# The causal convolution folded into the input projection on TensorE, and the routing weights computed on GpSimd, in a macaron block of MoE, Mamba and MoE

## The reference, cut to what matters

```
# FFN: 8 experts of 176 hidden, 2 per token, and a shared one of 352
router = xf @ Wg;  top_logits, idx = top_k(router, 2);  probs = softmax(top_logits)
w = zeros(n, 8).at[arange, idx].add(probs)
y = einsum('eth,ehc,te->tc', silu(xf W1) * (xf W2), W3, w) + (silu(xf Ws1) * (xf Ws2)) Ws3

# Mamba: inner width 256, state 16, 4 taps
xz = x @ W_in + b_in;  x_in, z = split(xz)
xt = causal_depthwise_conv(x_in, conv_w) + conv_b          # padded with 3 zeros on the left
x_conv = silu(xt)
Bm, Cm = split(x_conv @ W_xp + b_xp);  delta = softplus(x_conv @ W_dt + b_dt)
h = exp(delta*A) * h + delta*x_conv*Bm;  y = sum_s(h*Cm) + D_skip*x_conv
out = (y * silu(z)) @ W_out + b_out;  return layernorm(x + out) * alpha + beta
```

## Time and profile before

| | before |
|---|---|
| median of 3 runs | 2298.14 us (2297.28 to 2298.89) |
| the profiled execution | 2294.5 us, span 2292.7 us |
| mean granted clock of TensorE | 0.859 |
| busy: PE, DVE, ACT, POOL | 77%, 80%, 68%, 63% |
| instructions | 22561 |
| DMA | 299.53 MB, mean 131 GB/s |

### The profile page before, as it was taken

One profiled execution on the slowest core, in us unless ns is written; L12 is line 12 of the kernel. 1 busy time (PEld: TensorE's weight loads), 2 busy tenths in 40 slices (PEclk: granted clock), 3 DMA queues, 4 the chain that ended last, 5 costly groups with the idle time before them and its releaser, 6 DMA issues.

```text
span 2292.7 us, 22561 instructions
## 1 busy us (share of the span) xinstructions
PE 1759.5 (77%) x4416; PEld 770.7 (34%) x4416; DVE 1834.1 (80%) x2628; ACT 1554.5 (68%) x2114; POOL 1452.1 (63%) x1284
## 2 busy tenths in 40 slices
PE   4858488878788777787878787788778878876577
PEld 2323133333333333333333333333333333323233
DVE  1378989788897988979788897978979788888742
ACT  2449487776778677767776777777677867776522
POOL 3256676666576666666666666666666666676753
PEclk9879689788898889889898898988889888887688
DMA  4126655545554555546555554555455455546641
GB/s 127 51 79 152 143 137 150 136 121 132 145 139 124 148 133 142 130 122 161 133 129 133 135 139 122 144 139 133 124 139 149 127 143 132 132 118 166 151 106 60
DMA packets 118986, 299.53 MB, mean 131 GB/s; under 512 B 19168, under 2 KB 40384, under 8 KB 104512
## 3 DMA queue, kind: packets, MB, share of 16 engines
q0 software_dynamic: 18432, 125.84, 27.4%
q1 hardware_dynamic: 92672, 168.88, 23.3%
q10 hardware_dynamic: 7744, 3.57, 0.6%
HBM read 167.15 MB, written 5.24 MB: 75 GB/s over the span
## 4 chain that ended last, share of the span: by engine, by line
DVE 31%; PE 26%; ACT 18%; issue 18%; POOL 4%; DMA 1%; ACTq 1%; DVEq 1%; POOLq 0%
DVE hist L847 10%; PE ps_y L1027 6%; DVE ps_db L813 4%; PE ps_h2a L1032 4%; ACT L668 4%; ACT L645 3%; DVE dtmp L923 3%; PE ps_h1a L1014 3%; DVE den L891 3%; PE ps_h1b L1014 3%; PE ps_h2b L1032 2%; ACT decay L645 2%; DVE yacc L950 2%; ACT silu L668 2%; PE ps_m L1074 2%
## 5 line engine op out<-in xcount | busy, mean ns | idle before, releaser
L560 POOL TENSOR_TENSOR prod<-hist,crow 128x1024 f32<-128x1024 f32 x224 | 558.1, 2492 | 390.8 <-DVE hist L847 388.7
L847 DVE TENSOR_TENSOR_SCAN hist<-decay,ps_db 128x1024 f32<-128x1024 f32 x256 | 583.4, 2279 | 15.4 <-issue 12.8
L1027 PE MATMUL ps_y<-gated,down_w 128*128 128x512 f32 (+1 forms) x896 | 517.6, 664 | 96.0 <-POOL gated L512 64.0
L512 POOL TENSOR_TENSOR gated<-gated,silu 128x512 f32<-128x512 f32 x352 | 473.7, 1408 | 134.6 <-DVE gated L839 104.9
L813 DVE TENSOR_TENSOR ps_db<-du,ps_db 128x1024 f32<-128x1024 f32 x256 | 313.4, 1224 | 192.1 <-PE ps_db L996 190.0
L645 ACT ACTIVATE decay<-delta,a_neg 128x510 f32<-128x510 f32 x512 | 338.3, 711 | 2.6
L1032 PE MATMUL ps_h2a<-xnT,up_w 128*128 128x512 f32 (+1 forms) x448 | 259.2, 663 | 57.0 <-DVE gated L839 57.0
L1014 PE MATMUL ps_h1a<-xnT,up_w 128*128 128x512 f32 (+1 forms) x448 | 259.6, 663 | 50.0 <-ACT silu L668 48.8
L668 ACT ACT_TABLE_LOAD x229 | 293.8, 1283 | 5.3 <-PE ps_h1a L1014 1.2
L1032 PE MATMUL ps_h2b<-xnT,up_w 128*128 128x512 f32 x448 | 250.3, 642 | 53.6 <-DVE gated L839 53.6
L1027 PEld LDWEIGHTS ps_y<-gated,down_w 128*128 128x128 f32 (+1 forms) x896 | 181.6, 210 | 321.4 <-issue 211.9
(11 more groups left out here) (127 smaller groups left out, 2377.7 us busy)
## 6 DMA issues: line engine op xcount, KB each, us to landing
yacc<-prod POOLq DMA_DIRECT2D x112, 1024.0 KB, 8.9
crow<-c_rows SPq DMA_DIRECT2D x128, 512.0 KB, 4.1
wrow<-w_rows SPq DMA_DIRECT2D x320, 128.0 KB, 3.3
wrow<-w_rows SPq DMA_DIRECT2D x64, 224.0 KB, 3.1
wrow<-w_rows SPq DMA_DIRECT2D x64, 192.0 KB, 3.2
wrow<-w_rows SPq DMA_DIRECT2D x64, 160.0 KB, 3.2
yacc<-yacc POOLq DMA_DIRECT2D x16, 512.0 KB, 6.2
wrow<-w_rows SPq DMA_DIRECT2D x64, 96.0 KB, 3.0
```

What stands on the lines that cost most here:

```text
L512: nc.gpsimd.tensor_tensor(gated[:, pos % NGATE, :], gated[:, pos % NGATE, :], silu[:, (pos + NCHUNK * f_parity(k, f)) % NSILU, :], ALU.mul ...
L560: nc.gpsimd.tensor_tensor(prod[:, (pair - 1 + odd) % 2, s % 2, :, :], hist[:, s % 2, :, :], c_all, ALU.mult).then_inc(prod_done, 1)
L847: nc.vector.tensor_tensor_scan(hist[:, s % 2, :, :].rearrange("p h t -> p (h t)"), decay[:, s % NA, :, :, :].rearrange("p h b t -> p (h b ...
L1027: nc.tensor.matmul(ps_y[:], down_w[0:rd, jd, :], gated[0:rd, posd % NGATE, :], start=(posd == 0), stop=(posd == NCHUNK - 1)).then_inc(down ...
```

## The change

1. The four taps are folded into the weights of the input projection: at the start VectorE makes `w_conv[:, tap, :]` = `W_in` times the tap of each channel. `in0` and `in1` are then four matmuls each over the normed input, shifted by 0 to 3 tokens, that accumulate in `ps_m`, and a fifth over six columns that takes the bias of `b_in` back out where the padding stands. ScalarE's silu reads `ps_m` and writes `xconv`. The steps `conv0a` to `conv1b`, `xin` and the copy to it are gone; `dt0` and `xproj` wait for `in1` having been taken.
2. `weights0` and `weights1` run on GpSimd in the same slots, between the gated product and the state product of the slot; the reciprocal is a power of -1.
3. `wT` and `cT` become one buffer, `bounce`, to make room; each copy into it waits for the other's store.
4. At the start there are one more constant transfer (the taps, broadcast), six small operations on VectorE, two transposes and a copy for the fifth matmul's weights.

```diff
-        10: ["wT0", "conv0a"], 11: ["outT", "conv0b"], 12: ["resid"], 13: ["in1", "stats3"], 14: ["in2", "conv1a"],
-        15: ["in3", "conv1b", "ln_norm"], 17: ["y1"], 18: ["dt0", "stats1"], 19: ["dt1"], 20: ["yT1", "norm1"],
+        10: ["wT0"], 11: ["outT"], 12: ["resid"], 13: ["in1", "stats3"], 14: ["in2"],
+        15: ["in3", "ln_norm"], 17: ["y1"], 18: ["dt0", "stats1"], 19: ["dt1"], 20: ["yT1", "norm1"],
...
-        cT = sb("cT", [NS, TG])
+        bounce = sb("bounce", [NS, TG])
+        wT, cT = bounce[0:E, :], bounce
...
+                        elif step == "weights0" and enters(k) or step == "weights1" and tail(k):
...
+                            pool.wait_ge(edrop_ready, n + 1)
+                            chain.link(nc.gpsimd.tensor_tensor(den[:], edrop[:], pow_mone[:], ALU.subtract))
+                            chain.link(nc.gpsimd.tensor_tensor(prob[:, :, 0], den[:], pow_mone[:], ALU.pow))
+                            chain.link(nc.gpsimd.tensor_tensor(prob[:, :, 1], edrop[:], prob[:, :, 0], ALU.mult))
+                            pool.wait_ge(hot_ready, n + 1)
+                            chain.link(nc.gpsimd.tensor_tensor(
+                                hotp[:].rearrange("p t i e -> p (t i) e"), hot[:].rearrange("p t i e -> p (t i) e"),
+                                prob[:].rearrange("p t i -> p (t i)").unsqueeze(2).to_broadcast([P, TILES * 2, E]),
+                                ALU.mult))
+                            nc.gpsimd.tensor_tensor(wtok[:], hotp[:, :, 0, :], hotp[:, :, 1, :], ALU.add
+                                                    ).then_inc(wtok_ready, 1)
...
+                            held = k + 2 if step == "wT1" and lead(k) else k + 1
+                            if not isinstance(k, int) or 0 < held <= G:
+                                act.wait_ge(c_stored, 16 * held)
+                            nc.scalar.activation(wT, ps_m[0:E, :], ACT.Copy).then_inc(misc_taken, 1)
...
-                            nc.scalar.activation(xin[:, half, :, PAD:PAD + LEN],
-                                                 ps_m[:].rearrange("p (b t) -> p b t", b=NSEQ), ACT.Identity,
-                                                 bias=b_in_c[:, half:half + 1]).then_inc(misc_taken, 1)
+                            nc.scalar.activation(xconv[nxt][:, half, :], ps_m[:], ACT.Silu,
+                                                 bias=b_conv[:, half:half + 1]).then_inc(misc_taken, 1)
...
+            taps = taps_b.rearrange("p (c t) -> p t c", t=TAPS)
+            nc.vector.tensor_tensor(w_conv[:], w_in[:, 0:DI].unsqueeze(1).to_broadcast([P, TAPS, DI]), taps, ALU.mult
+                                    ).then_inc(taps_made, 1)
...
+            def convolved(half):
+
+                now = xnT[2][:].rearrange("p (b t) -> p b t", b=NSEQ)
+                acc = ps_m[:].rearrange("p (b t) -> p b t", b=NSEQ)
+                for tap in reversed(range(TAPS)):
+                    late = PAD - tap
+                    nc.tensor.matmul(acc[:, :, late:LEN], w_conv[:, tap, half * P:(half + 1) * P],
+                                     now[:, :, 0:LEN - late], start=(tap == PAD), stop=False)
+                return nc.tensor.matmul(acc[:, :, 0:PAD], edge_w[:, half * P:(half + 1) * P], edge[:],
+                                        start=False, stop=True)
...
-                            nc.tensor.matmul(ps_m[:], w_in[:, c * P:(c + 1) * P], xnT[2][:], start=True, stop=True
-                                             ).then_inc(misc_full, 1)
+                            if c < HALVES:
+                                convolved(c).then_inc(misc_full, 1)
+                            else:
+                                nc.tensor.matmul(ps_m[:], w_in[:, c * P:(c + 1) * P], xnT[2][:], start=True, stop=True
+                                                 ).then_inc(misc_full, 1)
```

More of the change, by code:

```diff
@@ L260, in macaron_kernel @@
         yT = sb("yT", [P, TG])
-        xin = sb("xin", [P, HALVES, NSEQ, PAD + LEN])
+        w_conv = sb("w_conv", [P, TAPS, DI])
+        b_tap = sb("b_tap", [P, HALVES, TAPS])
+        b_sum = sb("b_sum", [P, HALVES, 2])
+        b_conv = sb("b_conv", [P, HALVES])
+        edge_w = sb("edge_w", [PAD, DI])
+        edge = sb("edge", [PAD, NSEQ, PAD])
         xconv = [sb(f"xconv{i}", [P, HALVES, TG]) for i in range(2)]
@@ L730, in body @@
                                                  ).then_inc(misc_taken, 1)
-                        elif step in ("conv0b", "conv1b") and lead(k):
-                            half = int(step[4])
-                            act.wait_ge(conv_ready, HALVES * (k + 1) + half + 1)
-                            nc.scalar.activation(xconv[nxt][:, half, :],
-                                                 conv[:, half, :, :].rearrange("p b t -> p (b t)"), ACT.Silu,
-                                                 bias=conv_b_c[:, half:half + 1]).then_inc(xconv_ready, 1)
                         elif step in ("dt0", "dt1") and lead(k):
@@ L758, in _ @@
         def _(dve):
-            nc.vector.memset(xin[:, :, :, 0:PAD], 0.0).then_inc(pads_zero, 1)
             nc.vector.memset(decay[:, :, :, :, 0:1], 0.0).then_inc(pads_zero, 1)
@@ L817, in body @@
             def body(k, odd):
-                nonlocal route_chain, conv_chain, conv_last
                 nxt = 1 - odd
@@ L906, in body @@
                                                            ).then_inc(misc_taken, 1)
-                        elif step in ("conv0a", "conv1a") and lead(k):
-                            half = int(step[4])
-                            acc = conv[:, half, :, :]
-                            dve.wait_ge(misc_taken, turn(k, f"in{half}"))
-                            conv_chain = Chain(dve, dve_conv, TAPS - 1, HALVES * (k + 1) + half)
-                            conv_chain.link(nc.vector.tensor_scalar(acc, xin[:, half, :, 0:LEN],
-                                                                    conv_w_c[:, half, 0:1], None, ALU.mult))
-                            conv_last = nc.vector.scalar_tensor_tensor(acc, xin[:, half, :, 1:1 + LEN],
-                                                                       conv_w_c[:, half, 1:2], acc, ALU.mult, ALU.add)
-                        elif step in ("conv0b", "conv1b") and lead(k):
-                            half = int(step[4])
-                            acc = conv[:, half, :, :]
-                            for tap in range(2, TAPS):
-                                conv_chain.link(conv_last)
-                                conv_last = nc.vector.scalar_tensor_tensor(acc, xin[:, half, :, tap:tap + LEN],
-                                                                           conv_w_c[:, half, tap:tap + 1], acc,
-                                                                           ALU.mult, ALU.add)
-                            conv_chain.end()
-                            conv_last.then_inc(conv_ready, 1)
                         elif step == "delta" and lead(k):
@@ L978, in _ @@
             pe.wait_ge(consts_made, N_MADE)
+            pe.wait_ge(taps_made, 6)
+            for half in range(HALVES):
+                ins = nc.tensor.transpose(ps_m[0:PAD, half * P:(half + 1) * P], b_tap[:, half, 0:PAD], ident[:])
+            ins.then_inc(edge_full, 1)
+            pe.wait_ge(edge_made, 1)
             def claim(k, name):
```

70 lines of the change are left out of this document (37 added, 33 removed).

## The result

The changed kernel takes 2240.81 us (median of 4 runs, 2238.37 to 2245.37), the kernel before 2298.2 beside it (2297.28 to 2298.89): a ratio of 0.975, 95% interval 0.974 to 0.976. That is 57 us less, where 83 were forecast (2215). The profiled execution took 2238.37 us, its span is 2236.6.

A forecast was written before the change was run, and what follows sets the result against it. No engine was taken to fill the period; the bound changes hands along the 32 slots. From 2294.5 us, minus 60 and 34, plus 11, gave 2211.5, or 2215 as a median; range 2160 to 2270.

The forecast's parts named there:

- Part 1: Convolution on TensorE: 1.6 us from TensorE plus 2.4 from ScalarE, yT 4.0 us earlier in 15 groups, 60 us.
- ScalarE's part: Up to yT: ScalarE's 1.72 us wait for the last tap goes and silu replaces a copy, gain 2.4 us.
- start and end: Constant DMA, tap weights, lead-in body on TensorE, and uncontended weights in first and last body: 10.7 us added.
- The wait in slot 8 "stays": TensorE's 3.69 us wait for VectorE in slot 8, behind the gating of y, was to remain.
- (d): Rival: TensorE becomes the bound at a low clock in slots 9 to 14, about 2355 us; chance 0.08 with (e).
- Part 2: Routing weights on GpSimd: slot 8 gains nothing, in slot 28 wtok is 2.4 us earlier in 14 groups, 34 us.
- Edits at nothing: Shared buffer for wT and cT priced at nothing, covered by ScalarE's idle time; if uncovered, 3 us a group.
- (a): Rival: the low clock after yT goes too, 3 us a group, 2170 us; chance 0.15.
- (b): Rival: the whole of VectorE's time comes back, 18.5 us in 15 groups, 2031 us; chance 0.04.
- (c): Rival: a new TensorE wait drops the clock once in slots 9 to 17, costing 3 us a group, 2260 us; 0.13.
- (e): Rival: freed time is covered everywhere, only the ends count, 2309 us or no difference; chance 0.08 with (d).

The follow-up runs named there:

- r9: Kernel before, with twelve unread bf16 matmuls in each of four TensorE waits (slots 8, 18, 22, 29): 2274.84 us.
- r7: Changed kernel, with twelve unread bf16 matmuls in each of four TensorE waits (slots 8, 18, 22, 29): 2190.91 us.
- r3: Changed kernel with one tap's matmul in place of four, three taps left out of the computation: 2199.87 us.
- r1: Changed kernel with both routing-weight steps back on VectorE, so the fold of the convolution alone: 2233.53 us.
- r10: Fold of the convolution alone (weights on VectorE), with twelve unread matmuls in each of the same four TensorE waits: 2209.78 us.
- r5: Changed kernel with twelve unread bf16 matmuls in TensorE's wait for VectorE in slot 8 only: 2197.33 us.
- r2: Kernel before with only the routing weights moved to GpSimd: 2287.63 us.
- r6: Changed kernel with the second FFN's weights one slot earlier on GpSimd (27) and their transposes in slot 29: 2226.86 us.
- r8: Changed kernel with `weights0` (slot 8) alone back on VectorE: 2246.38 us.

## Why the prediction came out as it did

The sign, the bound and the order of size were right; the forecast was 26 us too low. The stages say where. The period is 132.0 us, not 130.4, and of the 4.56 us gained a group 3.12 lie in s4–s10, where the forecast had 4.0, and 1.29 between s14 and the next s4, where it had 2.4. In 15 and 14 groups that is 13 and 16 us, less 2 for the small gain in s10–s14. Both parts fell short, so the time lies inside the stated range without one error hiding another. r9 to r7, −84 us, looks like the forecast 83, but only because there two errors cancel: s4–s10 gains 5.9 and s14 to s4 gains 0.9.

**Part 1, TensorE bounds slots 9 to 14: right.** A folded half costs 3.0 us more (657.47 to 661.29 is 3.8, less 0.86), where 2.8 were taken. r3 showed that TensorE sets the end there. ScalarE's part, 2.4 us, was 2.45. VectorE's busy time fell by 341 us (300 or more was said), the input projection has 384 instructions and 82.5 us more (90 to 130 was said). One price was read across two measures: the 0.86 us of a matmul at the high clock is from one start to the next, the 2.08 at the low one is a duration, which is 1.02 at the high clock. From start to start it is 1.87 (649.19 to 651.06), so a low matmul costs 1.0 us more, not 1.2.

**The size of part 1: near for the fold alone, short in the whole change.** With its share of start and end it was 60 − 8.3 = 52 us; r1 gave 53 in the profiled execution and 66 in the median, with 4.5 us a group in s4–s10. In the whole change 3.1 were left, and with the waits filled it is 6.0 (55.81 in r9, 49.78 in r10). Most of the difference comes from one step: the count began at `ps_h1b` of slot 9 (658.63 in the earlier trace rows) and moved slot 8 as it was, 4.38 us from `ps_h2a` on. Slot 8 isn't a constant. It takes 5.28 or 4.12 us in the changed kernel and 2.58 in r5. A TensorE that isn't slowed there gains 1.8 more than the forecast had, out of the 2.0 by which 6.0 exceeds 4.0; one that is slowed longer loses 0.9. Of the 1.42 us a group between r1 and the whole change 0.96 lie in s4–s9 and 0.46 in s9–s10, behind the wait for `yT`.

**The wait in slot 8 "stays": right, and the costly word.** It is 3.56 us, and the low clock stays behind it. In before that cost nothing (r9); in the changed kernel it costs 43 us (r5), more than the 26 by which the forecast missed. The prediction knew that a low clock counts once TensorE is the bound, rival (d), but looked for it inside slots 9 to 14, where the clock was 1.00 as the earlier trace rows said, and not at their entrance.

**Part 2, 34 us: much too large, mainly by a price that the prediction had named and taken as covered.** With start and end it was 32 us; measured 12 alone (r2), 19 on the fold with the four waits filled, and nothing, or 7 us lost, without. Of the 2.4 us a group between s14 and the next s4 1.29 came. First, `wtok` came 2.0 us earlier against the scan of slot 28, not 2.4: GpSimd began at 610.10, which in the old count is 613.8 against 613.6, and `den` took 0.51 us in place of 0.2. The sum of the five, 2.6 us, was 0.3 over. Secondly, the prediction took `wT` to follow `wtok` as before. It came 1.0 earlier in this group and 1.2 in the mean of the twelve: the transposes at 613.29 stood in TensorE's order behind a down-projection of 1.91 us at half clock, and ran at it themselves (1.06 in place of 0.60). What would have shown it right, 2.4 us less idle ahead of `wT`, was 1.28. But this queue is not the larger part: in r6, with `wT` 1.7 us earlier, only 0.40 of the missing 1.1 came back. The larger part is the cover that the prediction relied on. It wrote that the gated product of slot 29 would come 2.3 us later, that TensorE's last down-projection waits for it, and that GpSimd's idle 4.54 us cover this. The product ends 7.6 us after s14 in before and in r1, and 10.1 in after, 2.5 later; GpSimd's idle time lies behind it and covers only GpSimd's own later work. The down-projection, which had no wait in before, now waits 1.92 us, and the next group's rows, up-projections and silu come behind it. No run takes this wait away, so its whole worth stays open; r6 shows that it is what remains once `wT` is early. The prediction's view of the Trainium skill's rule (GPSIMD Engine Reference, "Engine selection") stands halfway: the operations are slower on GpSimd, 2.6 us, and the move still paid alone (r2) and with the waits filled, since the same operations on VectorE stalled; the page SBUF — State Buffer ("Who interferes with whom") has VectorE and GpSimd sharing a port pair under a lock, and the trace agrees, since `den` took 5.51 us beside a gated product and 0.14 alone.

**Edits at nothing.** `weights0` on GpSimd in slot 8 cost nothing by r8. The shared bounce buffer shows no wait for a store.

**Start and end.** The first up-projection came 4.0 us later and the first scan 10.55, against 3.9 and 9.5 in the forecast's count; 1.3 us were added behind the last scan. Together that is 12, and 10.7 was forecast.

**The rivals.** (a) did not come: TensorE's wait for `yT` grew to 3.16 us; its price was near, s9–s10 shrinks by 2.5 with the waits filled, against 3. (b) did not come either, and r3 shows why: TensorE sets the end of these slots. (c) had the right mechanism, a low clock in this part of the group, but as a new wait; it was the old one, uncovered. (d) and (e) did not come as times; of (d) the mechanism, TensorE as the bound at a low clock, came at one place, slot 8.

## What to carry to other kernels

When work leaves the engine that sets the end, ask what of the next engine's slow stretches that work had covered, and count from the last wait that stays, not from the first instruction that changes. A TensorE that waits pays twice, in the wait and in the low clock behind it; before a further edit to a kernel whose chain TensorE leads, fill its longest waits with matmuls that nobody reads and see what they were worth. And for work that moves to another engine, follow what stands behind it in that engine's queue to whoever waits for it: here `wtok` came 2.0 us earlier and the gated product behind it 2.5 us later, and half of the gain was gone.

## What the runs showed of the hardware

The same instructions behind the same wait took 5.28 us in one group and 4.12 in the next, by where the granted clock rose from 0.50. So s4–s10 is 53.0 or 55.8 us in groups of the changed kernel and 50.0 or 52.9 in r5's. Executions of one program spread as well: r1 from 2225.67 to 2241.54 and r3 from 2184.95 to 2202.12, the kernel before by 7 to 8 us in each of the three later measurements. The Trainium skill (TensorE: Matmul & The Clock Gate, "The HAM clock gate") says that the number of slow matmuls at a kernel's start differs between runs of one kernel. No run here looked at the start; within one execution these traces show the like, from group to group.

2.6 us of idle-filling matmuls, once a group, shorten a kernel by 1.9% (r5 against after), and the same fill at the same place is worth nothing in the kernel before (s4–s9 43.59 against 43.53 in r9, which has it among its four).
